# Two product tiles between the last attention groups, the output bias on GpSimd, and an earlier rounding of the perceptron's result

## The reference

```python
for i in range(NUM_BLOCKS):                      # 4
    y = cond_layer_norm(x, cond, s1_w[i], s1_b[i], b1_w[i], b1_b[i])
    y = sparse_attention(y, src, dst, wq[i], bq[i], wk[i], bk[i], wv[i], bv[i], wo[i], bo[i])   # 4 heads; ends with out @ wo + bo
    x = x + y
    y = cond_layer_norm(x, cond, s2_w[i], s2_b[i], b2_w[i], b2_b[i])
    y = relu(y @ m_w1[i] + m_b1[i]) @ m_w2[i] + m_b2[i]
    x = x + y
```

## Time and profile before

| | |
|---|---|
| median of three runs | 3440.08 us (3434.08 to 3444.99) |
| the profiled execution | 3439.91 us, of which its span is 3438.6 us |
| PE busy | 3117.6 us, 91% of the span |
| DVE / ACT / POOL busy | 2186.7 / 1408.4 / 1254.6 us |
| granted TensorE clock, mean | 0.971 |

### The profile page before, as it was taken

The page is one execution under the profiler, slowest core; times in us unless marked ns, Lnnn a source line. Parts: engine busy times, 40 slices in busy tenths (PEclk is TensorE's granted clock), DMA queues, the critical chain, the costliest instruction groups (busy, mean ns, idle before and its releaser), DMA issues.

```text
span 3438.6 us, 42149 instructions
## 1 busy us (share of the span) xinstructions
PE 3117.6 (91%) x14851; PEld 2230.3 (65%) x14872; DVE 2186.7 (64%) x4808; ACT 1408.4 (41%) x2135; POOL 1254.6 (36%) x1035
## 2 busy tenths in 40 slices
PE   5899898998978788999998999999999999999998
PEld 2333476444752235866446988778977898778987
DVE  6989522788347774243455768756785576657776
ACT  6888733000341013333144545334542455325544
POOL 3666335777357774442201012411223111331022
PEclk8999998999999999999999999999999999999999
DMA  3555442767337764223102011220012101130012
GB/s 83 161 160 166 131 149 70 215 198 202 86 99 210 210 200 137 79 82 131 40 26 75 7 35 34 70 68 13 32 46 89 40 7 62 43 95 7 7 62 73
DMA packets 137281, 318.29 MB, mean 93 GB/s; under 512 B 25380, under 2 KB 43108, under 8 KB 136046
## 3 DMA queue, kind: packets, MB, share of 16 engines
q0 software_dynamic: 53040, 173.84, 17.7%
q1 hardware_dynamic: 82590, 139.10, 12.8%
q10 hardware_dynamic: 1440, 2.62, 0.2%
HBM read 269.50 MB, written 24.84 MB: 86 GB/s over the span
## 4 chain that ended last, share of the span: by engine, by line
PE 73%; DVE 14%; issue 6%; ACT 3%; DVEq 2%; DMA 1%; POOL 1%; SPq 1%; POOLq 0%; ACTq 0%
PE bank L140 15%; PE bank L142 15%; PE bank L141 15%; PE bank L792 10%; PE bank L2274 5%; DVE G L913 4%; PE bank L802 3%; PE bank L1992 2%; PE bank L1636 2%; PE bank L770 1%; DVE y_tile L1944 1%; DVE y_tile L1946 1%; DVE x_stats L1927 1%; DVEq L861 1%; ACT G L779 1%
## 5 line engine op out<-in xcount | busy, mean ns | idle before, releaser
L792 PE MATMUL bank<-gathered,selector 128*128 128x512 f32 x1326 | 668.0, 619 | 130.8 <-DVE G L913 88.9
L913 DVE TENSOR_TENSOR G<-G,bank 128x512 f32 x663 | 453.8, 684 | 167.9 <-PE bank L792 94.8
L792 PEld LDWEIGHTS bank<-gathered,selector 128*128 128x128 f32 x1326 | 217.7, 193 | 423.6 <-issue 369.1
L1301 POOL TENSOR_TENSOR weight_parts<-weight_ring,weight_parts 128x512 fp32r<-128x512 f32 x136 | 201.3, 1481 | 392.9 <-ACT weight_parts L1273 392.9
L2346 ACT CAST probT<-bank 128x512 fp32r<-128x512 f32 (+1 forms) x480 | 216.2, 524 | 270.5 <-PE bank L2274 270.5
L1289 DVE TENSOR_TENSOR lhs_parts<-G,lhs_parts 128x640 fp32r<-128x640 f32 x128 | 107.2, 838 | 340.4 <-ACT lhs_parts L1271 340.2
L2420 DVE CUSTOM_DVE_ANT_0 prob<-bank,count_by_src 128x512 f32<-128x512 f32 (+1 forms) x480 | 258.4, 588 | 91.3 <-PE bank L142 91.3
L779 ACT COPY G<-bank 128x512 f32<-128x512 f32 x160 | 81.2, 654 | 546.7 <-PE bank L770 546.7
L818 ACT ACTIVATE sign_src<-node_iota_16bit,src_float 128x1280 bf16<-128x1280 f16 x208 | 282.3, 1361 | 49.4 <-PE bank L802 43.6
L140 PE MATMUL bank<-weight_parts,lhs_parts 128*128 128x512 f32 x680 | 271.6, 399 | 33.6 <-POOL weight_parts L1301 30.9
L2352 DVE TENSOR_TENSOR probT<-bank,probT 128x512 fp32r<-128x512 f32 (+1 forms) x480 | 258.9, 595 | 53.6 <-ACT probT L2346 53.6
(11 more groups left out here) (278 smaller groups left out, 6902.1 us busy)
## 6 DMA issues: line engine op xcount, KB each, us to landing
weight_ring<-in_L_gnn_basis SPq DMA_DIRECT2D x64, 256.0 KB, 2.7
weight_ring<-in_L_gnn_bases SPq DMA_DIRECT2D x64, 256.0 KB, 2.6
x_L<-x_rows SPq DMA_DIRECT2D x50, 256.0 KB, 4.5
x_rows<-x_L SPq DMA_DIRECT2D x40, 256.0 KB, 2.0
yT_hi<-yT_new_hi SPq DMA_DIRECT2D x4, 2560.0 KB, 10.8
yT_lo<-yT_new_lo SPq DMA_DIRECT2D x4, 2560.0 KB, 10.9
count_rows<-count SPq DMA_DIRECT2D x10, 640.0 KB, 6.6
count_by_dst<-count_rows SPq DMA_DIRECT2D x10, 640.0 KB, 8.9
```

The source lines that it names most:

```text
L792: pe.matmul(bank[s % banks][:], sel[:, s % SELECTORS, :], xs[:, s % slots, :], start=True, stop=True).then_inc(*multiplied.inc())
L913: dve.tensor_tensor(g, g, bank[s % banks][:], ALU.add).then_inc(*added.inc())
```

## The change

Four things are done:

- **Two tiles ahead.** Products 0 and 1 of the odd joins move from the join into the attention's last head: on PE, product 0 stands before the turn of tile 9, product 1 between the second half of group 3 and group 4. Their rounding on ACT stands behind the exponentials of tiles 7 and 8. DVE's addition of product 0 (with its mean and variance) stands between the leaving of groups 3 and 4, with the wait for the reloaded `x` in front of it. PE's wait for all groups moves to tile 2 of the join.
- **The bias on GpSimd.** `bo` is no longer added by DVE at the head of the odd join. POOL adds it to the ten tiles of `x` in `project_values`, in place, from rows of its own (`output_bias_rows`, loaded with the values' bias), as soon as the layer-norm has read `x`. So `x` is stored after that, in `project_values`, and in block 0 too, where the start value was reloaded before. SP issues the ten stores between its two `yT` copies, each behind POOL's addition; `project_first` on ACT waits for all ten.
- **Rounding sooner.** In `multiply_hidden`, the first two tiles of the even join are rounded behind the eighth relu, which ends the second span; PE's product 0 then waits for the eleventh relu (bank 0), product 1 for the twelfth.
- Each tile's rounding waits for the group or span that it reads, no longer for all.

```diff
@@ join(s)
         def on_pe():
-            pe.wait_ge(*outer_split(s))
...
-            if s % 2:
-                pe.wait_ge(*left(QUERY_GROUPS * HEADS * (i + 1)))
             for j in range(NT):
-                multiply(j)
+                if j >= ahead(s):
+                    multiply_tile(s, j)
                 if s < LAST:
                     condition(s, j)
+                    if j == 2 and s % 2:
+                        pe.wait_ge(*left(QUERY_GROUPS * HEADS * (i + 1)))
                     if j >= 2:
                         turn_tile(s, j - 2)
...
         def on_act():
-            act.wait_ge(*(left(QUERY_GROUPS * HEADS * (i + 1)) if s % 2 else relued(HID * (i + 1))))
-            part_lhs(0)
-            part_lhs(1)
             for j in range(NT):
                 if j + 2 < NT:
-                    part_lhs(j + 2)
+                    part_lhs(s, j + 2)
...
         def on_dve():
-            if s % 2:
-                dve.wait_ge(*bias_in(3 * (i + 1)))
-                dve.wait_ge(*x_back(NT * (i + 1)))
-                for j in range(NT):
-                    dve.tensor_tensor(x[:, j, :], x[:, j, :], bias_rows[:, 0, :], ALU.add).then_inc(*biased.inc())
-            dve.wait_ge(*biased.now())
+            if s % 2 == 0:
+                dve.wait_ge(*biased.now())
             for j in range(NT):
-                dve.wait_ge(*product(p + j + 1))
-                dve.tensor_tensor(x[:, j, :], x[:, j, :], bank[j % 2][:], ALU.add).then_inc(*added.inc())
-                dve.wait_ge(*added.now())
-                measure_tile(j)
+                if j or s % 2 == 0:
+                    add_tile(s, j)
...
+    def ahead(s):
+        return 2 if s % 2 else 0
+
+    def multiply_tile(s, j):
+        i, p = (s - 1) // 2, (s - 1) * NT
+        if j == 0:
+            pe.wait_ge(*outer_split(s))
+        if j < 2:
+            pe.wait_ge(*(masked(3 * NT * HEADS * (i + 1)) if s % 2 else relued(HID * (i + 1) - 2 + j + 1)))
+        else:
+            pe.wait_ge(*added(p + j - 2 + 1))
+        pe.wait_ge(*lhs_lo(p + j + 1))
+        for k in range(KC):
+            ins = split_matmul(pe, bank[j % 2][:], [lhs_parts[:, j % 2, q, k, :] for q in range(2)],
+                               [part[:, k, :] for part in (outer_hi, outer_lo)], k == 0, k == KC - 1)
+        ins.then_inc(*product.inc())
+
+    def part_lhs(s, j):
+        i, p = (s - 1) // 2, (s - 1) * NT
+        if j >= 2:
+            act.wait_ge(*product(p + j - 2 + 1))
+        if s % 2:
+            act.wait_ge(*left(QUERY_GROUPS * (HEADS * (i + 1) - 1) + j // PER_GROUP + 1))
+        else:
+            act.wait_ge(*relued(HID * i + KC * (j // 4 + 1)))
+        act.copy(lhs_parts[:, j % 2, 0], attnT[:, :, j * P:(j + 1) * P]).then_inc(*lhs_hi.inc())
@@ project_values(i)
             sp.dma_start(yT[0][:].bitcast(F32), yT_new[0][:].bitcast(F32)).then_inc(*copied.inc())
+            for j in range(NT):
+                sp.wait_ge(*out_biased(NT * i + j + 1))
+                sp.dma_start(tile_rows(x_rows, j), x[:, j, :]).then_inc(*x_spilled.inc())
             sp.wait_ge(*values(NT * (i + 1)))
...
+        def on_pool():
+            pool.wait_ge(*out_bias_in(i + 1))
+            if i == 0:
+                pool.wait_ge(*C.x_start_stored.now())
+            for j in range(NT):
+                pool.wait_ge(*normed(g + j + 1))
+                pool.tensor_tensor(x[:, j, :], x[:, j, :], out_bias[:], ALU.add).then_inc(*out_biased.inc())
@@ project_first(i)
-            act.wait_ge(*(x_spilled(NT * i) if i else C.x_start_stored.now()))
+            act.wait_ge(*x_spilled(NT * (i + 1)))
@@ attention(i)
                 else:
+                    multiply_tile(2 * i + 1, 0)
                     turn(h, NT - 1)
                     values_of(h, 3, 5, NT)
+                    multiply_tile(2 * i + 1, 1)
                     values_of(h, 4, 0, NT)
...
+                    if h == HEADS - 1 and t in (7, 8):
+                        part_lhs(2 * i + 1, t - 7)
...
-                    for group in (3, 4):
-                        leave(h, group)
+                    leave(h, 3)
+                    dve.wait_ge(*x_back(NT * (i + 1)))
+                    add_tile(2 * i + 1, 0)
+                    leave(h, 4)
@@ multiply_hidden(i)
                                bias=mb[:, o:o + 1]).then_inc(*relued.inc())
+                if u == 2 * KC - 1:
+                    part_lhs(s + 1, 0)
+                    part_lhs(s + 1, 1)
@@ begin_block(i)
-        if i:
-            for j in range(NT):
-                sp.wait_ge(*added(NT * (2 * i - 1) + j + 1))
-                sp.dma_start(tile_rows(x_rows, j), x[:, j, :]).then_inc(*x_spilled.inc())
```

More of the change, by code:

```diff
@@ L1762, in layer_3 @@
     V_hi = M.new("value_parts_hi", [P, 2, NP], F32R)
+    out_bias = M.new("output_bias_rows", [P, D])
     bias_place = M.at
@@ L1785, in layer_3 @@
     M.at = bias_place
-    bias_rows = M.new("bias_rows", [P, 2, D])
+    bias_rows = M.new("bias_rows", [P, D])
     M.at = C.x_place
@@ L1839, in layer_3 @@
     C.x_start_stored = C.landed("x_stored")
+    out_bias_in, out_biased = C.landed("edges_in"), C.event("weight_lo")
     hidden_tiles = [(m, o) for m in range(len(SPANS)) for o in range(KC)]
@@ L2150, in join, with add_tile @@
         on_dve()
+    def ahead(s):
[14 more added lines that the diff above has]
+    def part_lhs(s, j):
+        i, p = (s - 1) // 2, (s - 1) * NT
+        if j >= 2:
[5 more added lines that the diff above has]
+        act.copy(lhs_parts[:, j % 2, 0], attnT[:, :, j * P:(j + 1) * P]).then_inc(*lhs_hi.inc())
+    def add_tile(s, j):
+        dve.wait_ge(*product((s - 1) * NT + j + 1))
+        dve.tensor_tensor(x[:, j, :], x[:, j, :], bank[j % 2][:], ALU.add).then_inc(*added.inc())
+        dve.wait_ge(*added.now())
+        measure_tile(j)
     def turn_tile(s, j):
@@ L2450, in on_sp @@
             load_product_weight(1, "L3_gnn_m_w1", i)
-            for stage, n in enumerate(("bo", "m_b2")):
-                sp.dma_start(bias_rows[:, stage, :], broadcast(A["L3_gnn_" + n][i:i + 1, :], D)).then_inc(*bias_in.inc())
+            sp.dma_start(bias_rows[:], broadcast(A["L3_gnn_m_b2"][i:i + 1, :], D)).then_inc(*bias_in.inc())
             sp.dma_start(mb[:], A["L3_gnn_m_b1"][i:i + 1, :].rearrange("a (k p) -> p (a k)", p=P),
@@ L2455, in on_sp @@
             sp.wait_ge(*scored(NT * end))
-            sp.wait_ge(*(x_spilled(NT * i) if i else C.x_start_stored.now()))
+            sp.wait_ge(*x_spilled(NT * (i + 1)))
             for j in range(NT):
-                sp.dma_start(x[:, j, :], tile_rows(x_rows if i else C.x1_rows, j)).then_inc(*x_back.inc())
+                sp.dma_start(x[:, j, :], tile_rows(x_rows, j)).then_inc(*x_back.inc())
         def split_values_of(h):
@@ L2511, in on_act @@
                                bias=mb[:, o:o + 1]).then_inc(*relued.inc())
+                if u == 2 * KC - 1:
+                    part_lhs(s + 1, 0)
+                    part_lhs(s + 1, 1)
         def on_dve():
+            dve.wait_ge(*bias_in(2 * (i + 1)))
             dve.wait_ge(*normed(g + NT))
             for j in range(NT):
[L2516 removed]
+                dve.tensor_tensor(x[:, j, :], x[:, j, :], bias_rows[:], ALU.add).then_inc(*biased.inc())
             if i == BLOCKS - 1:
```

24 lines of the change are left out of this document (6 added, 18 removed).

## The result

| | before | after |
|---|---|---|
| median, same chip | 3437.24 us (3434.08 to 3444.99, 4 runs) | 3402.68 us (3398.8 to 3403.89, 4 runs) |
| ratio | | 0.9894, 95% interval 0.9874 to 0.9914 |
| the profiled execution, its span | 3439.91, 3438.6 us | 3402.41, 3401.1 us |
| PE / DVE / POOL busy | 3117.6 / 2186.7 / 1254.6 us | 3101.6 / 2159.2 / 1311.4 us |

The change is faster by 1.1%. The medians of the same chip are 34.6 us apart. The two profiled executions are 37.5 us apart where the forecast had 29.8; some 3 us of the difference between these figures is that the profiled execution of before was slower than its median of four.

A forecast was written before the change was run, and what follows sets the result against it. PE, busy 91% of the span, was taken as the bound, so time is won where it stands or runs slow. The sum was 3439.9 - 24.2 (odd joins) - 10.6 (even joins) + 5.0 (block 0) = 3410.1 us, range 3401 to 3423.

The forecast's parts named there:

- the odd join, 24.2 us: Odd joins: two tiles of products ahead and the bias gone add tile 2 6.05 us sooner a block, 24.2 in four.
- even join, 10.6 us: Even joins: sooner rounding removes PE's whole gap of 2.65 us before each, 10.6 us in four.
- Block 0's +5.0: Block 0 before its attention: POOL's additions colliding with mask steps, and stores queued behind yT_hi, lose 5.0 us.
- rival C: Block 0 costs nothing, as stores share DMA engines with yT_hi and DVE yields little; 3405 us, chance 0.09.
- 22.0 us behind the last scores: Sign in the odd join: DVE adds tile 2 22.0 us behind the last scores' end, where it was 28.05.
- what follows keeps its order and its distances: Even join: after the 2.65 us gap goes, later work is unchanged in order and spacing.
- 4 to 6 given as the sign: Sign in block 0: PE stands 4 to 6 us before the first key part, in the other blocks not.
- A: Odd joins: product 2 falls to the half clock after its gap, 1.6 us a block more; 3417 us, chance 0.13.
- B: Block 0: POOL's chain holds the mask up to 13 us; 3417, up to 3422 us with slow stores, chance 0.12.
- D: All four blocks: project_first waits for the stores, making the kernel slower than before; 3448 us, chance 0.03.
- E: Odd joins: product 0 doesn't fill the gap, PE stands before the turn, 2 us a block more; 3418, chance 0.03.
- the upper bound: Block 0: POOL's whole chain of additions holds DVE's mask for 13 us, costing up to 12 us.

The follow-up runs named there:

- e2: The kernel before with only the even join's earlier rounding added; 0.9951 of the time of before.
- e4: The changed kernel with block 0's bias additions on POOL held back until the mask is made; 0.9876 of the time of before.
- e5: The changed kernel with block 0's ten stores of x put ahead of the first yT copy on SP's queue; 0.9887 of the time of before.
- e10: The changed kernel run again, unaltered, on another run's chip; 3404.07 us, 0.9901 of the time of before.
- e7: The changed kernel with the bias added by DVE inside the attention's end and the stores where they were before; 0.9908 of the time of before.
- e3: The changed kernel without tiles ahead and without the earlier rounding, leaving only the bias on GpSimd and its stores; 1.0005 of the time of before.
- e1: The changed kernel with the even join's rounding put back behind the perceptron; 0.9929 of the time of before.

## Why the prediction was right, and which terms were off

The mechanism held at each place but one, the later tiles of the even join. What was off is the size of three terms of the sum, all in the same direction. The step that failed is the adding up of the odd join, 24.2 us, and of the even join, 10.6 us, both too small: the stretches gave 27.7 and 13.7. Block 0's +5.0 was too large. The measured 3402.7 lies nearer to rival C's 3405 than to 3410, yet C's mechanism is not what happened: block 0 did cost its time.

**The odd join, 6.05 us a block, measured 6.9 (27.7 in four instead of 24.2).** This is the term with the largest error. By the trace, shifted by 3.05 us to before's time (product 0 starts at 2104.92 instead of 2101.87), tile 1 is added at 2117.22 where the working had 2117.9, and tile 2 at 2120.35 where it had 2121.2. Of these 0.85 us, 0.44 are PE's: I added the lengths of its groups end to end, but a group starts about 0.16 before the modelled end of the one ahead of it, so each insertion between groups costs that much less (group 4 ended at 2114.38, not 2114.82). The rest lies in ACT's and DVE's chain behind it, which I also added end to end (its terms make 2117.8, and I wrote 2117.9), and in 3.13 instead of 3.23 us from tile 1 to tile 2. Some of the 6.9 us is the clock. Before, product 0 ran at 0.50 and DVE stood 0.70 us for product 1 behind it. In e2's block 3 product 0 happened to take 4.57 instead of 5.46 us, DVE did not stand there, and that odd join was 0.8 to 1.0 us shorter than its three neighbours. The working had this inside the step from the old tile 2 to the new, without naming it. The 22.0 us behind the last scores, given as the sign, became 21.17.

**The even join, 2.65 us a block, measured 2.9 plus 0.7.** The gap went whole, and about 0.2 is once more the overlap of two groups. The step that failed here is "what follows keeps its order and its distances". It kept its order. The distances changed, and by the timelines with the POOL work that falls beside DVE's: `x_shift` of tile 1, one column wide, took 0.94 us before and 0.42 after. e2 shows it too, 37.7 to 38.0, without the rest of the change. Join 8, which has no modulation, has no such rest (33.26, 33.34) and gained the gap alone. Together 13.7 us instead of 10.6.

**Block 0, +5.0, measured +4.1.** In four more executions of the same code it was +2.8 to +3.3 against the same 54.66. Both halves were there, and e4 and e5 part them. The following is of the pair with +4.1. The mask was late by 3.1 us (the 1.99 of `yT_hi`'s issue and the 1.12 by which layer 3 began sooner), 3.5 forecast. The stores ended 18.1 us behind that issue (ACT began at 1861.20), 18.8 forecast. The first key part stood at 1862.73, in before's time 1863.85, which is 4.0 later than in the earlier trace rows; the working had 1864.9. PE stood 1.7 us in front of it and not the 4 to 6 given as the sign, because the slower values had already brought PE there some 2 us later; that figure counted the same time twice.

**The chip's own part.** -1.1 us ahead of layer 3 and +1.0 in the middle heads, neither of which the change touches, cancel.

**The rivals.** A (product 2 at half clock) did not happen, 1.00 in the windows of this product in all four blocks and again in e10. e7 shows a fall in three blocks of four behind a wait 0.3 us longer, but a smaller one (4.58 us at 0.63, not 5.4), and DVE was late itself there, so the join lost at most 0.2 us by it. A's price of 1.6 a block was not seen in any run. B (the mask held up by the whole chain) is out: the mask was 3.1 us late, not the 10 or so that B's price needs. C (block 0 free) is out by 2.8 to 4.1 us. D (a wait for the stores in every block) had the stores land some ten microseconds ahead of their need. An addition took 1.25 us on POOL, 3.9 was the point from which it decides. E is out, with no idle ahead of product 0.

The Trainium skill (SBUF — State Buffer, "Who interferes with whom") has the first issuer block the other for the whole of its instruction. The 3.74 us of the earlier trace rows agree with that much: DVE's addition ended 0.54 us behind GpSimd's instruction. My extending it to a whole chain of GpSimd instructions, as the upper bound, is what failed: the mask steps took 1.95 to 2.57 us instead of 1.48 and the additions 1.97 instead of 1.25, so no mask step was held longer than one addition takes, by these lengths the two took turns, and e4 restores both numbers (1.48 and 1.25).

**What stays open.** Why DVE's small instructions meet POOL's less often after the earlier rounding was read from the timelines, not tried. The 0.4 us won behind group 4 in the odd join are read off, not isolated. Nor is it known what sets block 0's spread of 1.3 us, nor what decides whether the clock falls.

## What to carry to other kernels

Filling a gap is worth only what it does for the instruction that ends the stage: product 0 ahead of the turn bought time, product 1 ahead of the last group cost 0.9 us a block, and work is better placed behind the group whose end starts the next chain. Work taken from one engine gains nothing while the wait that it covered remains (e3: 8.25 us of additions gone, 1.6 gained in the odd join, and a slow clock in the even one took that back), so an edit of two halves has to be costed as one. When additions are moved to GpSimd, look for what VectorE reads from SBUF in the same microseconds, and hold them back until it is done. A single stretch of a single execution is no measure of 1 us unless the same code has been seen to repeat it: block 0's did not, the odd join's did.

## What the runs showed of the hardware

**The clock after a gap is not decided by the gap's length alone.** A gap of 1.49 us was followed by 1.00 in all odd joins of the change. In e7 one of 1.81 us was followed by a product at 0.63 in three blocks, and one of 1.79 by 1.00 in the fourth. One of 2.65 was followed by 1.00 in the even joins of before and in three of e1's, and by 0.63 in e1's block 2 and in all of e3's. What decides between them I can't read from these rows.

**The same code falls to the lower clock in one execution and not in the next.** These are windows of block 2's values products behind the same gap of 2.09 us, in the changed kernel's second profile (e10), where the stretch was 49.05 us:

```profile
2623.00:2625.00 2.00, 2.00 (x7) 1.52 (x6) 0.00 (x0) 0.00 (x0) 2.00 (x3) 0.50 1.07 317
```

and in its first, where it was 47.53:

```profile
2622.80:2625.00 2.20, 2.17 (x9) 1.79 (x10) 0.48 (x1) 0.00 (x0) 2.20 (x3) 1.00 1.04 302
```

0.50 is 1.2 GHz. The fall costs 1.5 us. In e10's own blocks 1 and 3, behind the same gap of 2.09 us, the stretch was 47.52. e10's layer 3 took 1592.9 us and that of the first profile 1588.8, and three longer stretches (1.5, 1.7 and 0.8 us) are the difference. The first two had a fall; the third ran at full clock and PE waited 1.22 instead of 0.41 us for a modulated tile. So a step worth 1 us is read from stretches that had none, not from the total.
